# Attention stage: head halves paired on the same partitions, GpSimd doing the rotary add, and logits as 64x64 tiles

## The reference, cut to what matters

```python
def _apply_rope(x, positions):
    ...
    x1, x2 = jnp.split(x, 2, axis=-1)
    return jnp.concatenate([x1 * cos - x2 * sin, x2 * cos + x1 * sin], axis=-1)
...
q = jnp.einsum('BTD,NDH->BTNH', xn, q_w)          # B 16, T 1024, D 512, N 4 heads, H 128
kv = jnp.einsum('BSD,cKDH->cBSKH', mn, kv_w)      # S 64 keys, one head of keys and values
q = _apply_rope(q, q_pos) * HEAD_DIM ** (-0.5)
k = _apply_rope(k, k_pos)
logits = jnp.einsum('BTKGH,BSKH->BKGTS', q, k)
probs = jax.nn.softmax(jnp.where(mem_mask, logits, MASK_FILL), axis=-1)
enc = jnp.einsum('BKGTS,BSKH->BTKGH', probs, v)
x = x + jnp.tanh(g_xattn) * jnp.einsum('BTNH,NHD->BTD', enc, out_w)
```

## Time and profile before

| | |
|---|---|
| median of 3 runs | 2039.99 us (2036.7 to 2043.06) |
| the profiled execution, its own time | 2038.99 us |
| span of its instructions | 2037.2 us |
| busy in the span | PE 1826.3 (90%), DVE 1413.5 (69%), ACT 876.4 (43%), POOL 260.2 (13%) |
| TensorE's granted clock over the span | 0.973 of full speed |
| from about 75 to 850 us | attention stage |

### The profile page before, as it was taken

One profiled execution on the slowest core, in us unless ns is written; L12 is line 12 of the kernel. 1 busy time (PEld: TensorE's weight loads), 2 busy tenths in 40 slices (PEclk: granted clock), 3 DMA queues, 4 the chain that ended last, 5 costly groups with the idle time before them and its releaser, 6 DMA issues.

```text
span 2037.2 us, 53514 instructions
## 1 busy us (share of the span) xinstructions
PE 1826.3 (90%) x23504; PEld 1282.2 (63%) x23504; DVE 1413.5 (69%) x2114; ACT 876.4 (43%) x1126; POOL 260.2 (13%) x624
## 2 busy tenths in 40 slices
PE   6699999999999999868889988998888898889885
PEld 3377777777777777656665566566656665665551
DVE  4177777777777777634776668667756766686666
ACT  2533333333333333235445544544554454545531
POOL 0122222222222222101100110111011001100100
PEclk9799999999999999979999999999999999999997
DMA  7412323333332323135645765575457547655752
GB/s 233 171 52 95 115 95 118 113 122 116 119 116 95 115 95 128 50 132 226 248 158 198 270 224 170 211 270 217 156 210 265 188 169 253 240 178 187 270 183 88
DMA packets 123814, 339.24 MB, mean 167 GB/s; under 512 B 10304, under 2 KB 18240, under 8 KB 106176
## 3 DMA queue, kind: packets, MB, share of 16 engines
q1 hardware_dynamic: 123584, 335.82, 46.2%
HBM read 259.23 MB, written 76.55 MB: 165 GB/s over the span
## 4 chain that ended last, share of the span: by engine, by line
PE 37%; DVE 7%; DMA 5%; issue 4%; ACT 3%; SPq 0%; POOL 0%; DVEq 0%
PE ps L1024 13%; PE ps L998 7%; PE ps L969 4%; PE ps L1062 4%; DMA out<-y 4%; PE ps L1045 4%; DVE res L924 3%; PE ps L963 3%; DMA y<-x_scratch 1%; PE ps L1058 1%; DVE gat L885 1%; PE ps L1059 1%; DVE res L879 1%; ACT gat L825 1%; ACT gat L820 1%
## 5 line engine op out<-in xcount | busy, mean ns | idle before, releaser
L879 DVE STREAM_TRANSPOSE res<-res 128x2048 f32<-128x2048 f32 x128 | 292.1, 2295 | 0.1
L820 ACT ACTIVATE gat<-ps 128x1536 f32<-128x1536 f32 (+1 forms) x128 | 172.2, 1345 | 222.8 <-PE ps L998 222.8
L892 DVE SCALAR_TENSOR_TENSOR y<-ps,gate_f,y 128x512 f32<-128x512 f32 x128 | 95.2, 744 | 209.5 <-DMA y<-x_scratch 152.4
L559 PE MATMUL ps<-xTh,qh 128*128 128x512 f32 x512 | 203.0, 397 | 1.4 <-DVE xTl L486 1.4
L1024 PE MATMUL ps<-gat,ring 128*64 128x64 f32 x5120 | 176.7, 227 | 27.4 <-issue 27.3
L559 PE MATMUL ps<-xTh,ql 128*128 128x512 f32 x512 | 200.6, 392 | 0.0
L559 PE MATMUL ps<-xTl,qh 128*128 128x512 f32 x512 | 200.4, 391 | 0.0
L1024 PEld LDWEIGHTS ps<-gat,ring 128*64 128x64 f32 x5120 | 163.7, 141 | 38.0 <-issue 30.6
L998 PE MATMUL ps<-sel,xn 32*128 32x128 f32 x4096 | 154.9, 286 | 31.7 <-ACT sel L842 18.6
L998 PEld LDWEIGHTS ps<-sel,xn 32*128 32x128 f32 x4096 | 131.1, 188 | 67.3 <-ACT gat L820 43.1
L924 DVE COPY res<-ps 128x1024 f32<-128x1024 f32 x128 | 151.7, 1220 | 20.1 <-PE ps L1045 19.7
(11 more groups left out here) (117 smaller groups left out, 3268.2 us busy)
## 6 DMA issues: line engine op xcount, KB each, us to landing
ring<-in_W SPq DMA_DIRECT2D x80, 1024.0 KB, 5.7
gat<-in_W SPq DMA_DIRECT2D x48, 1024.0 KB, 9.3
xin<-in_x SPq DMA_DIRECT2D x32, 1024.0 KB, 5.8
x_scratch<-xin SPq DMA_DIRECT2D x32, 1024.0 KB, 4.3
xn<-x_scratch SPq DMA_DIRECT2D x64, 512.0 KB, 6.4
y<-x_scratch SPq DMA_DIRECT2D x128, 256.0 KB, 3.9
out<-y SPq DMA_DIRECT2D x128, 256.0 KB, 3.9
vw_scratch<-cx SPq DMA_DIRECT2D x16, 512.0 KB, 2.6
```

Of the source, the lines that this page charges most:

```text
L559: last = e.matmul(ps[:, 2 + n % 2, :], a[:, c, n * DH:(n + 1) * DH], b[:, c, :], start=(k == 0), stop=(k == len(parts) - 1))
L820: e.activation(o, v, ACT.Copy).then_inc(m_gaA.sem, 1)
L879: e.transpose(v, v).then_inc(m_tr.sem, 1)
L892: e.scalar_tensor_tensor(out=v, in0=ps[:, 4 + t % 4, :], scalar=gate_f[:], in1=v, op0=ALU.mult, op1=ALU.add).then_inc(m_fin.sem, 1)
```

## The change

The host puts the query weights' columns in another order: of each pair of heads (a, b), one column block now holds the first half of a and the second half of b, and the next the second half of a and the first half of b. The two halves that a turn combines then lie on the same partitions of two blocks. The sign in the sine table fits both.

- GpSimd gets four instructions of 128x512 a unit, for each pair `qc[2p] -= qs[2p+1]` and `qc[2p+1] += qs[2p]`, behind its two products `pr`, with a new mark `m_rot`.
- `logits` runs once a unit, on `qc` alone and over 64 partitions a call: eight calls with weights of 64x64 and 512 columns. For k (the half of the keys) there are four calls, one for each combination of input half h and output half h^p, into bank 3+p. On one set of partitions the two banks are different; each bank is written from both input halves, on different partitions. It waits for all four GpSimd instructions (`m_rot`) and for `m_pl` of the unit before.
- ACT copies both banks in one instruction of 128x1024 instead of two of 128x512.
- PSUM banks: `logits` 3 and 4, `logits_T` 0 and 1, `probs_T` 7 and 4, `values` 5 and 6. The waits follow.
- The order by hand is new on TensorE, DVE and ACT. The prologue takes the output weights of the second pair in swapped order.

```diff
@@ gpsimd, behind the two products pr of unit g
+                if unit(g + 1):
+                    for p in range(2):
+                        e.wait_ge(m_qs.sem, m_qs.at(g + 1, 2 * p + 1))
+                        e.tensor_tensor(qc[:, 2 * p, :], qc[:, 2 * p, :], qs[:, 2 * p + 1, :], ALU.subtract).then_inc(m_rot.sem, 1)
+                        e.tensor_tensor(qc[:, 2 * p + 1, :], qc[:, 2 * p + 1, :], qs[:, 2 * p, :], ALU.add).then_inc(m_rot.sem, 1)
@@ scalar
-            def logits(u, p):
-                e.wait_ge(m_L.sem, m_L.at(u, p))
-                e.activation(lt[:, p, :], ps[:, 4, :], ACT.Identity, scale=float(DH) ** -0.5,
+            def logits(u):
+                e.wait_ge(m_L.sem, m_L.at(u))
+                e.activation(lt[:], ps[:, 3:5, :], ACT.Identity, scale=float(DH) ** -0.5,
...
@@ vector, one pass
-                if unit(g + 1):
-                    turned(g + 1, 0)
                 if unit(g):
                     sums(g, 0)
                     sums(g, 1)
                 if unit(g + 1):
+                    turned(g + 1, 0)
                     turned(g + 1, 1)
-                    turned(g + 1, 2)
...
                 if unit(g + 3):
                     stats(g + 3, 0)
+                if unit(g + 1):
+                    turned(g + 1, 2)
+                if unit(g):
+                    probs_lo(g, 0)
+                    probs_lo(g, 1)
+                if unit(g + 3):
                     stats(g + 3, 1)
                 if unit(g + 1):
                     turned(g + 1, 3)
...
@@ tensor
-            def logits(u, p):
-                e.wait_ge(m_qs.sem, m_qs.at(u, 2 * p + 1))
-                if p:
-                    e.wait_ge(m_lt.sem, m_lt.at(u, 0))
-                elif u:
-                    e.wait_ge(m_lt.sem, m_lt.at(u - 1, 1))
+            def logits(u):
+                e.wait_ge(m_rot.sem, m_rot.at(u, 3))
+                if u:
+                    e.wait_ge(m_pl.sem, m_pl.at(u - 1, 1))
...
                 for k in range(2):
-                    for n in range(2):
-                        last = e.matmul(ps[n * S:(n + 1) * S, 4, :], kb[:, b % 2, k * S:(k + 1) * S],
-                                        (qc, qs)[k][:, 2 * p + n, :], start=(k == 0), stop=(k == 1))
+                    for p in range(2):
+                        for h in range(2):
+                            r, o = slice(h * S, (h + 1) * S), slice((h ^ p) * S, ((h ^ p) + 1) * S)
+                            last = e.matmul(ps[o, 3 + p, :], kb[r, b % 2, k * S:(k + 1) * S], qc[r, 2 * p + k, :],
+                                            start=(k == 0), stop=(k == 1))
@@ tensor, one pass
                 if unit(g + 1):
-                    queries(g + 1)
+                    for n in range(3):
+                        queries(g + 1, n)
+                if unit(g):
+                    probs_T(g, 0)
+                    probs_T(g, 1)
+                if unit(g + 1):
+                    queries(g + 1, 3)
                 if unit(g + 2):
                     turn(g + 2, 0)
                     turn(g + 2, 1)
-                if unit(g + 1):
-                    logits(g + 1, 0)
                 if unit(g):
-                    probs_T(g, 0)
+                    values(g, 0)
+                    values(g, 1)
                 if unit(g + 2):
                     turn(g + 2, 2)
                     turn(g + 2, 3)
                 if unit(g + 1):
-                    logits(g + 1, 1)
+                    logits(g + 1)
                 if unit(g):
-                    probs_T(g, 1)
-                    for t in range(TH):
-                        values(g, t)
+                    values(g, 2)
+                    values(g, 3)
@@ kernel (host)
+    qa, qb = np.asarray(L0_xattn_q_w)[:, :, :DH // 2], np.asarray(L0_xattn_q_w)[:, :, DH // 2:]
+    qp = np.stack([np.concatenate(h, axis=1) for n in (0, 2) for h in ((qa[n], qb[n + 1]), (qb[n], qa[n + 1]))])
```

More of the change, by code:

```diff
@@ L416, in probs @@
                 e.wait_ge(m_PT.sem, m_PT.at(u, tp))
-                e.activation(pTh[:, tp, :], ps[:, 7, :], ACT.Copy).then_inc(m_pT.sem, 1)
+                e.activation(pTh[:, tp, :], ps[:, 7 - 3 * tp, :], ACT.Copy).then_inc(m_pT.sem, 1)
             for g in range(-2, NU):
@@ L438, in _ @@
                     e.activation(vw[:, b % 2, 0], vraw[:], ACT.Copy).then_inc(m_vh.sem, 1)
-                if unit(u):
-                    hi(u, 0)
-                    hi(u, 1)
-                if unit(g + 1):
-                    logits(g + 1, 0)
                 if unit(g):
                     probs(g, 0)
+                    probs(g, 1)
                 if unit(u):
-                    hi(u, 2)
-                    hi(u, 3)
+                    for c in range(C):
+                        hi(u, c)
                 if unit(g + 1):
-                    logits(g + 1, 1)
-                if unit(g):
-                    probs(g, 1)
+                    logits(g + 1)
         @blk.vector
@@ L457, in top_of @@
                 e.wait_ge(m_LT.sem, m_LT.at(u, tp))
-                e.tensor_reduce(out=mx[:, tp, :], in_=heads(ps[:, 5 + tp, :]), op=ALU.max, axis=AX_X).then_inc(m_mx.sem, 1)
+                e.tensor_reduce(out=mx[:, tp, :], in_=heads(ps[:, tp, :]), op=ALU.max, axis=AX_X).then_inc(m_mx.sem, 1)
                 e.wait_ge(m_mx.sem, m_mx.at(u, tp))
@@ L489, in probs_lo @@
                 e.wait_ge(m_pT.sem, m_pT.at(u, tp))
-                e.tensor_tensor(pTl[:, tp, :], ps[:, 7, :], pTh[:, tp, :].bitcast(F32), ALU.subtract).then_inc(m_pl.sem, 1)
+                e.tensor_tensor(pTl[:, tp, :], ps[:, 7 - 3 * tp, :], pTh[:, tp, :].bitcast(F32), ALU.subtract).then_inc(m_pl.sem, 1)
             def add(u, t):
                 e.wait_ge(m_PV.sem, m_PV.at(u, t))
-                e.tensor_tensor(xin[:, u % RING, t, :], ps[:, t % 2, :], xin[:, u % RING, t, :], ALU.add).then_inc(m_rs.sem, 1)
+                e.tensor_tensor(xin[:, u % RING, t, :], ps[:, 5 + t % 2, :], xin[:, u % RING, t, :], ALU.add).then_inc(m_rs.sem, 1)
             for g in range(-3, NU):
@@ L520, in _ @@
                 if unit(g):
-                    probs_lo(g, 0)
+                    add(g, 0)
+                    add(g, 1)
+                if unit(g + 3):
+                    stats(g + 3, 2)
+                    stats(g + 3, 3)
                 if unit(g + 2):
@@ L524, in _ @@
                     lo(g + 2, 3)
[L525 to L533, removed]
                 u = g + 3
@@ L548, in _, with queries @@
         def _(e):
[L549 to L561, removed]
+            def queries(u, n):
+                if n >= 2:
+                    e.wait_ge(m_qs.sem, m_qs.at(u, n - 2))
+                else:
+                    e.wait_ge(m_lo.sem, m_lo.at(u, C - 1))
+                    if u:
+                        e.wait_ge(m_qs.sem, m_qs.at(u - 1, n + 2))
+                        e.wait_ge(m_lt.sem, m_lt.at(u - 1))
+                parts = [(a, b, c) for c in range(C) for a, b in ((qh, xTh), (qh, xTl), (ql, xTh))]
+                for k, (a, b, c) in enumerate(parts):
+                    last = e.matmul(ps[:, 2 + n % 2, :], a[:, c, n * DH:(n + 1) * DH], b[:, c, :],
+                                    start=(k == 0), stop=(k == len(parts) - 1))
+                last.then_inc(m_Q.sem, 1)
             def turn(u, c):
@@ L600, in probs_T @@
                 e.wait_ge(m_pr.sem, m_pr.at(u, tp))
[L601 to L604, removed]
+                if u:
+                    e.wait_ge(m_pl.sem, m_pl.at(u - 1, tp))
                 for k in range(4):
-                    last = e.transpose(ps[:, 7, k * P:(k + 1) * P], pr_[:, tp, k * P:(k + 1) * P], ident[:])
+                    last = e.transpose(ps[:, 7 - 3 * tp, k * P:(k + 1) * P], pr_[:, tp, k * P:(k + 1) * P], ident[:])
                 last.then_inc(m_PT.sem, 1)
@@ L611, in values @@
                     e.wait_ge(m_rs.sem, m_rs.at(u, t - 2))
-                elif unit(u + 2):
-                    e.wait_ge(m_lo.sem, m_lo.at(u + 2, 2 + t))
-                else:
+                elif u:
                     e.wait_ge(m_rs.sem, m_rs.at(u - 1, 2 + t))
@@ L620, in values @@
                     column = (2 * (t % 2) + p) * P
-                    last = e.matmul(ps[:, t % 2, :], a[:, t // 2, column:column + P], vw[:, u // 2 % 2, k, p, :],
+                    last = e.matmul(ps[:, 5 + t % 2, :], a[:, t // 2, column:column + P], vw[:, u // 2 % 2, k, p, :],
                                     start=(m == 0), stop=(m == len(parts) - 1))
```

31 lines of the change are left out of this document (16 added, 15 removed).

## The result

The changed kernel takes 2016.99 us (median of four runs, 2002.38 to 2021.56) against 2039.74 us before; the ratio is 0.9876, 95% interval 0.9835 to 0.9917. Forecast were 2001 us and a range of 1985 to 2035. So the change gains 1.2 to 1.4%, where 1.9% was forecast.

A forecast was written before the change was run, and what follows sets the result against it. TensorE was taken to set the pace at 24.05 us a unit, then the second loop at 22.83: 28 units gain 34.2 us, four others 6.6, filling costs 2.4, together 38.4 off 2039.0, giving 2001 us, range 1985 to 2035.

The forecast's parts named there:

- The tiles run at once: Logits on TensorE: four 64x64 tiles run together, so one block costs two steps, 1.87 us, and 1.87 is gained.
- Rival 1: Logits: PSUM banks collide, tiles run two at a time, block 3.74 us; 23 us slower, 2062; chance 0.12.
- The second loop: From one last add to the next, through store, load, DVE, GpSimd and logits: 22.83 us, above TensorE's 22.18.
- Rival 2: TensorE keeps the pace, as loads land earlier or the loop has more room; 22.18 + 0.2, 1989 us; chance 0.08.
- last add to the statistics (store, load): SP stores a unit and loads a new one before DVE's first statistics: 10.2 us of the loop.
- statistics to GpSimd's third instruction: DVE's part of the loop: statistics 0.60 twice, third head 1.20, two `pTl` 1.21, fourth head up to its end 1.28.
- GpSimd's third and fourth instruction: GpSimd's last two instructions in the loop: 2.04 us, from 1.04 for `pr` with the same element count.
- hand-over, logits, values, last add: End of the loop: logits block 1.87, `values` 2 and 3 2.84, last add 0.20 + 0.69, handing over 0.1 in all.
- filling: One-time cost at the first unit: two GpSimd instructions (2.04) and the longer ACT copy (0.33) unhidden, 2.4 us.
- the other units: The four units without a load run at TensorE's 22.18 plus 0.2 of small waits, gaining 6.6 us.
- Rival 3: GpSimd's add of two full inputs is slow or slowed by DVE; at double price 27 us slower, 2066; chance 0.07.
- about 3: DVE's idle time per unit ahead of the first statistics, waiting for the load of x, in us.

The follow-up runs named there:

- e8: Changed kernel's order, banks and waits with the old logits, no GpSimd instruction, weights in old order; ratio 1.0011 to the kernel before.
- e2: Changed kernel with DVE's first two statistics of the new unit moved behind the fourth head's products; 1993.1 us, ratio 0.9755 to the kernel before.
- e3: Changed kernel with a ring of five units of x instead of four, loads issued a unit earlier; 1998.0 us, ratio 0.9771 to the kernel before.
- e5: Changed kernel without GpSimd's four instructions, cross terms of the turn left out; 1991.1 us, ratio 0.9759 to the kernel before.
- e6: Changed kernel with GpSimd's four instructions in four different forms, computing other values; 2005.2 us in one run.
- e1: Changed kernel run again without an edit; 2014.4 us, ratio 0.9859 to the kernel before.
- e4: As e2, with the first head's products also ahead of the sums; 1985.2 us, ratio 0.9711 to the kernel before.

## Why the prediction was right, and where its size was off

**The tiles run at once: right.** The block was to take 1.87 us and takes 1.88. Rival 1, the collision of banks, would have made it 3.74. By the rule of the Trainium skill (TensorEngine Tiling (Array Packing), "Gotcha 1: PSUM Pressure") that different row tiles can't access one bank simultaneously, no gain was to be had. The measurement decides against it for tiles on different partitions of the bank: eight calls, each bank written from both input halves, in 1.88 us, where the same number of records in e8, two tiles at a time, takes 3.59. The skill's other page (PSUM — Partial Sum Buffer, "PSUM bank collisions raise a hardware error"), by which each bank of each partition is a RAM of its own, agrees with this. The same section also quotes the rule on row tiles, and there too the measurement decides; that two row tiles in one bank and on the same 32 partitions collide, as it adds, no run here shows.

**The second loop becomes the pace: right.** The prediction had 22.83 us; the loop's parts in the trace add up to 23.08 (means over 26 units), and the unit is 23.04. e2 and e3 take the load out and e5 takes GpSimd out, and each leaves TensorE's own 22.3 to 22.4. Rival 2, in which TensorE keeps the pace at once at 22.38, was wrong by 0.66 us a unit.

**The terms of the loop, one by one:**

| part of the loop | predicted us | measured us | over 28 units |
|---|---|---|---|
| last add to the statistics (store, load) | 10.2 | 9.88 | -9 |
| statistics to GpSimd's third instruction | 4.89 + 0.05 | 4.95 | 0 |
| GpSimd's third and fourth instruction | 2.04 | 2.52 | +13 |
| hand-over, logits, values, last add | 0.05 + 5.60 | 0.06 + 5.67 | +2 |
| sum | 22.83 | 23.08 | +7 |

The mis-sized term is GpSimd's. The step that failed was: "I take 1.04, as the element count is the same". The element count was the wrong thing to go by; `pr` reads 8 values over and over as its second input, and e6 shows 1.045 us for that form beside 1.28 to 1.29 for those with a full second input. The prediction had named just this doubt and let it into the range, not into the sum. The estimate by the Trainium skill (GPSIMD Engine Reference, "3.1 Elementwise — side-by-side cycle accounting"), 1.12 us, was nearer than the row, and still short by 0.17.

The load's term was off the other way. The row of before had 5.8 us from issue to landing; the changed kernel's own:

```profile
L365 SPq DMA_DIRECT2D xin<-in_x x28: 372/378/384, 142.1 to 765.0; - x28
...
DMA to landing us min/median/max: 5.1/5.4/5.8
```

The longer term hid the shorter one in part. That the two partly cancel is luck, not skill of the sum. Why the load lands 0.4 us sooner was not tried.

**Gain by stage.** Of 38.4 us forecast for attention 31.5 came. 28 units gain 1.01 in place of 1.22, 5.8 us less; filling, the other units and the drain gave 3.1 in place of 4.2. The remaining 8.6 us of the first profile lie outside, and most of them are the scatter of the experts stage: in e1 the median falls by 28.7 us with an attention stage 30.5 us shorter, in e4 by 57.9 with 57.8. In e2, e3 and e5 it falls by 4 to 6 us less than the attention stage, so that some us outside attention stay open.

**What lay beside it.** ACT's one copy of 1024 columns took 1.11 instead of 1.02, from the end of the logits at 411.26 to 412.37, with TensorE's transposes at 414.02: still hidden. DVE stood idle 3.14 us for the load in the unit shown, as "about 3" said, but in the units with the values' difference only 0.1 to 0.9, so 47 us in all and not near 90; the prediction counted that instruction at its 1.2 us of before, and beside GpSimd it takes 2.28. Even by its own numbers, 10.2 less 6.7 and 10.2 less 7.9 in turns, the wait came to 81 us and not 90. TensorE waited 0.6 us a unit for GpSimd, as written.

Rival 3 said that slow GpSimd instructions turn the sign from 1.65 us each. At 1.26 each (2.52 for both) they took 13 of the 38.4 us forecast, a third, and not the sign.

## What to carry to other kernels

When a change takes work off the engine that sets the pace, write down the next longest loop with its waits, up to the load that an engine issues only after its last result: here it was 22.83 us by the prediction, 95% of a unit before, and it kept 0.77 us (23.04 against e2's 22.27) of the 1.87 us a unit that TensorE had freed. If an engine in order has an instruction that waits for a load, put it behind the work that someone else waits for; moving the first two statistics gave 1.1% here (e2 against e1). For the price of an instruction not yet in the trace, match the inputs' shapes too, not only the element count.

## What the runs showed of the hardware

- **Two tiles with different input halves write the same PSUM bank at once,** here on different partitions: 1.88 us for eight calls of 64x64 with 512 columns, the time of two steps. The same partitions were not tried.
- **GpSimd's two-input instruction takes longer with a second full input:** 1.29 us for 128x512 fp32, 1.045 with 8 values repeated 64 times each (e6).
- **DVE and GpSimd shut each other out, for whole instructions, where both read two inputs from SBUF.** In the changed kernel's timeline DVE's difference of the values starts 0.09 us behind a GpSimd instruction and takes 2.28 us instead of 1.22; the GpSimd instruction behind it then takes 2.27 instead of 1.29:

```profile
421.95 1.29 POOL L385 TENSOR_TENSOR qc<-qc,qs 128x512 f32<-128x512 f32 x1 [1.43 <-DVE qs L477]
422.04 2.28 DVE L511 TENSOR_TENSOR vw<-vraw,vw 128x1024 fp32r<-128x1024 f32 x1 [0.17 <-ACT vw L446]
423.20 2.27 POOL L386 TENSOR_TENSOR qc<-qc,qs 128x512 f32<-128x512 f32 x1
```

In e4's timeline DVE comes first by 0.04 us, and GpSimd alone pays:

```profile
412.79 1.23 DVE L512 TENSOR_TENSOR vw<-vraw,vw 128x1024 fp32r<-128x1024 f32 x1
412.83 2.34 POOL L385 TENSOR_TENSOR qc<-qc,qs 128x512 f32<-128x512 f32 x1
415.12 1.30 POOL L386 TENSOR_TENSOR qc<-qc,qs 128x512 f32<-128x512 f32 x1
```

In e6 the GpSimd instruction that starts in front of DVE's is the short form of 1.045 us, 0.24 shorter, and DVE's instruction takes 2.03 us, 0.25 less than beside the long form, as it would if it had to wait for the other's end:

```profile
L514 DVE TENSOR_TENSOR vw<-vraw,vw 128x1024 fp32r<-128x1024 f32 x15 | 30.4, 2030 | 2.6 <-ACT vw L449 2.6
```

DVE's instructions with one input in PSUM kept their 0.64 to 0.69 us beside GpSimd's, in every trace looked at.
